# Two graph layers on one core: x·W0a taken ahead of the tiles, x·(W0b+1)+b between them, other edge values, one search for foreign entries per group

## The reference

```
deg = sum(adj, axis=1)
y   = concat([adj @ x / deg, x], axis=1) @ W0 + b
x1  = layernorm(x + y)                      # over the 128 columns, no gain, no offset
h   = x1 @ W.T
e   = (h @ a[:128])[:, None] + (h @ a[128:])[None, :]
p   = softmax(where(adj == 0, -inf, e), axis=1)
out = layernorm(x1 + p @ h)
```

## Time and profile before

| what | value |
|---|---|
| median of 3 runs | 1074.1 us |
| the profiled execution: its own time, its span | 1073.98 us, 1072.3 us |
| its mean granted TensorE clock | 0.993 |
| TensorE busy | 998.3 us (93%), 8777 instructions |
| VectorE, ScalarE, GpSimd busy | 728.6, 601.0, 310.3 us |
| adj loads | 36864 packets, 268.45 MB |

### The profile page before, as it was taken

One profiled execution on the slowest core, in us unless ns is written; L12 is line 12 of the kernel. 1 busy time (PEld: TensorE's weight loads), 2 busy tenths in 40 slices (PEclk: granted clock), 3 DMA queues, 4 the chain that ended last, 5 costly groups with the idle time before them and its releaser, 6 DMA issues.

```text
span 1072.3 us, 22059 instructions
## 1 busy us (share of the span) xinstructions
PE 998.3 (93%) x8777; PEld 868.2 (81%) x8777; DVE 728.6 (68%) x1722; ACT 601.0 (56%) x533; POOL 310.3 (29%) x333
## 2 busy tenths in 40 slices
PE   0778888989999999999999999999999999999996
PEld 0566677777888888888888888888888888888885
DVE  4797888888978877777666665555534655656654
ACT  5677788888888778776767675656521100000000
POOL 5445344454544443433333333322000000000000
PEclk9999999999999999999999999999999999999999
DMA  9999999999999999999989888879230022222011
GB/s 324 422 421 420 402 409 416 416 417 422 407 421 412 417 395 396 385 386 364 357 346 330 336 325 322 318 314 360 83 127 7 19 71 85 85 85 72 26 41 32
DMA packets 51594, 305.36 MB, mean 285 GB/s; under 512 B 6560, under 2 KB 7840, under 8 KB 17952
## 3 DMA queue, kind: packets, MB, share of 16 engines
q0 software_dynamic: 36864, 268.45, 63.1%
q1 hardware_dynamic: 12672, 33.06, 8.8%
q10 hardware_dynamic: 1952, 2.39, 0.8%
HBM read 286.29 MB, written 17.59 MB: 283 GB/s over the span
## 4 chain that ended last, share of the span: by engine, by line
PE 81%; DMA 9%; ACT 4%; issue 2%; DVE 2%; POOL 1%; ACTq 0%; DVEq 0%; POOLq 0%
PE ps_agg L315 48%; PE ps_part L315 24%; DMA adj_in<-in_adj_dram,chunk 8%; PE ps_y L315 4%; ACT edges L452 3%; PE ps_y L591 1%; PE ps_y L590 1%; POOL adj_in L1144 1%; DMA x_all<-in_x_dram 1%; PE ps_h L598 1%; DVE edgesT L754 1%; PE ps_catT L579 0%; PE ps_x1T L585 0%; PE ps_catT L580 0%; DVE edgesT L751 0%
## 5 line engine op out<-in xcount | busy, mean ns | idle before, releaser
L315 PE MATMUL ps_agg<-parts,edgesT 128*128 128x257 f16 (+1 forms) x5312 | 616.7, 275 | 34.6 <-DVE edgesT L754 30.9
L315 PEld LDWEIGHTS ps_agg<-parts,edgesT 128*128 128x128 fp8e4 x5312 | 520.6, 98 | 119.2 <-DVE edgesT L754 35.7
L452 ACT ACTIVATE edges<-adj_in 128x4096 fp8e4<-128x4096 int32 x126 | 455.4, 3614 | 32.5 <-DMA adj_in<-in_adj_dram,chunk 31.8
L1144 POOL DMA_INDIRECT adj_in<-in_adj_dram,chunk x256 | 260.9, 1019 | 440.3 <-ACT edges L452 387.5
L315 PE MATMUL ps_part<-parts,edgesT 128*128 128x258 f16 x1664 | 194.6, 273 | 0.0
L315 PEld LDWEIGHTS ps_part<-parts,edgesT 128*128 128x128 fp8e4 x1664 | 162.7, 98 | 22.7
L763 DVE SCALAR_TENSOR_TENSOR stray<-edgesT,stray 128x1024 uint32<-128x1024 uint32 x128 | 158.4, 1238 | 0.5
L522 ACT ACTIVATE std<-mean_var,eps 128x1 f32<-128x1 f32 x64 | 18.9, 295 | 204.0 <-DVE mean_var L977 204.0
L458 ACT ACTIVATE catT<-ps_catT 128x256 f32<-128x256 f32 x64 | 24.6, 384 | 159.2 <-PE ps_catT L580 145.0
L751 DVE STREAM_TRANSPOSE edgesT<-edges 128x512 uint32<-128x512 uint32 x128 | 89.9, 702 | 16.6 <-ACT edges L452 13.4
L315 PE MATMUL ps_part<-parts,packed 128*128 128x258 f16 x836 | 96.4, 273 | 0.0
(11 more groups left out here) (100 smaller groups left out, 696.9 us busy)
## 6 DMA issues: line engine op xcount, KB each, us to landing
adj_in<-in_adj_dram,chunk POOLq DMA_INDIRECT x256, 8.8
out_dram<-edges SPq DMA_DIRECT2D x60, 64.0 KB, 2.9
partial_sums<-partial SPq DMA_DIRECT2D x13, 258.0 KB
adj_in<-partial_sums SPq DMA_DIRECT2D x13, 258.0 KB, 6.0
packed_adj<-packed SPq DMA_DIRECT2D x3, 1024.0 KB
x_all<-in_x_dram SPq DMA_DIRECT2D x8, 256.0 KB, 8.4
x_all<-in_x_dram ACTq DMA_DIRECT2D x8, 256.0 KB, 8.9
adj_in<-packed_adj SPq DMA_DIRECT2D x2, 1024.0 KB, 6.8
```

Of the source, the lines that this page charges most:

```text
L315: done = eng.matmul(bank[:, 0:cols], rows[:, n // BYTES, n % BYTES, :], moving[:, n, :], start=(n == first), stop=(n == last))
L452: act.activation(edges[:, half, :, :], adj_in[:, n % SLOTS, :, :], ACT.Copy, scale=2.0 if t % GROUP == GROUP - 1 else 1.0, saturate=False) ...
L1144: pool.indirect_dma_start(adj_in[:, n % SLOTS, r, :], None, adj_chunks, bass.IndirectOffsetOnAxis(chunk[:, 0:1], 0), element_offset=first_ ...
```

## The change

1. `parts0` holds the split of 4096·u, u = x·W0a, in place of x. Ahead of the tiles, for each of 16 groups j of four blocks: four transposes of x (`transpose_x`), one copy by ScalarE (`copy_xT`), four products with W0a (`dense`), the high part by ScalarE (`split_u`), the low part by VectorE (`split_u_lo`).
2. v = x·(W0b+1)+b takes x's place in `x_all`. Groups 0 and 1 are made ahead (`dense_self`, `keep_v`), groups 2 to 15 in the odd tiles 1 to 27: four transposes ahead of first_layer(t), four products behind it, a ScalarE copy and a VectorE addition.
3. Per tile, transpose_cat, the catT copy, project and add_bias are gone. z = (agg + low part + v) comes in two VectorE instructions straight from `ps_agg`; all row work is one tile earlier.
4. An edge is 128.0, or 192.0 in every fourth tile. Kept bits are 0x10, 0x20, 0x40 and 0x04; bits 0x8B are kept along in `packed`, and are searched for only there, once per group (2 instructions in place of 8). Every tile is packed at full width; the stores keep their sizes. The unpack of every fourth tile shifts and masks.
5. The first adj tile is converted and transposed after steps 10, 12, 14 and 15 of the work ahead. GpSimd begins to load adj when the first quarter of x has landed. The first four blocks of x and W0 are loaded first; VectorE transposes both halves of a tile together at the head of its step; extremes of u are taken in tiles 40 to 52.

```diff
+        FIRST_AFTER = [10, 12, 14, 15]
+        AHEAD = 2
+        def late_group(t):
+            j = (t + 3) // 2
+            return j if t % 2 == 1 and AHEAD <= j < GROUPS else None
...
         @block.scalar
+            for j in range(GROUPS + 1):
+                if j < GROUPS:
+                    copy_xT(j)
+                if j > 0:
+                    split_u(j - 1)
+                if j in FIRST_AFTER:
+                    convert_first(FIRST_AFTER.index(j))
             act.wait_ge(s_w1T, 1)
...
-                if on(t, 1):
-                    copy_catT(t - 1)
-                if on(t, 3):
-                    copy_x1T(t - 3)
+                if on(t, 2):
+                    copy_x1T(t - 2)
+                if late_group(t) is not None:
+                    copy_late_xT(late_group(t))
...
-                if on(t, 2):
-                    deviation(t - 2)
+                if on(t, 1):
+                    deviation(t - 1)
...
         @block.tensor
+            for j in range(GROUPS + 1):
+                if j < GROUPS:
+                    transpose_x(j)
+                if j == 1:
+                    pe.wait_ge(s_const, 16)
+                if j > 0:
+                    dense(j - 1)
+                if 0 < j <= AHEAD:
+                    dense_self(j - 1)
...
             def first_layer(t):
                 pe.wait_ge(s_trh, 2 * t + 2)
-                wait(pe, s_aggr, t - 1)
+                wait(pe, s_z, t - 1)
+                if t == 0:
+                    pe.wait_ge(s_lo0, GROUPS)
...
-                if on(t, 1):
-                    transpose_cat(t - 1)
-                if on(t, 3):
-                    transpose_x1(t - 3)
+                if on(t, 2):
+                    transpose_x1(t - 2)
+                if late_group(t) is not None:
+                    late_transpose_x(late_group(t))
                 first_layer(t)
-                if on(t, 1):
-                    project(t - 1)
-                if on(t, 3):
-                    hidden(t - 3)
+                if on(t, 2):
+                    hidden(t - 2)
+                if late_group(t) is not None:
+                    late_dense_self(late_group(t))
...
         @block.vector
             def step(t):
-                if on(t, 0):
+                if on(t, 0) and t > 0:
                     transpose_half(t, 0)
+                    transpose_half(t, 1)
                 if on(t, 1):
                     degree(t - 1)
+                    residual_lo(t - 1)
+                    residual(t - 1)
...
                 if on(t, 0):
-                    check_and_pack(t)
+                    pack(t)
+                if on(t, 1) and (t - 1) % GROUP == GROUP - 1:
+                    check((t - 1) // GROUP, 0)
+                if on(t, 2) and (t - 2) % GROUP == GROUP - 1:
+                    check((t - 2) // GROUP, 1)
+                if late_group(t) is not None:
+                    keep_v(late_group(t))
...
         @block.gpsimd
-            pool.wait_ge(s_x[1], 16 * NQ)
-            for n in range(SLOTS):
+            pool.wait_ge(s_x[0], 16 * NQ)
+            for n in range(2 * TILES):
                 load_half(n)
```

More of the change, by code:

```diff
@@ L438, in _ @@
[L438 to L441, removed]
-            act.wait_ge(s_fill, 1)
[L443 to L446, removed]
+                    first = 1 if s == 0 else 0
@@ L452, in convert @@
                 act.activation(edges[:, half, :, :], adj_in[:, n % SLOTS, :, :], ACT.Copy,
[L453 to L458, removed]
+                               scale=EDGE[t % GROUP], saturate=False).then_inc(s_conv, 1)
             def copy_x1T(t):
@@ L567, in first_layer @@
                 pe.wait_ge(s_trh, 2 * t + 2)
-                wait(pe, s_aggr, t - 1)
[L569 to L580, removed]
+                wait(pe, s_z, t - 1)
+                if t == 0:
+                    pe.wait_ge(s_lo0, GROUPS)
+                if t == 1:
+                    pe.wait_ge(s_vkept, AHEAD)
+                contract(pe, ps_agg[t % 2], edgesT[:, t % 2, :], parts0[:, :, 0:2 * F + 1],
+                         range(NBLK), 0, NBLK - 1).then_inc(s_agg, 1)
             def transpose_x1(t):
@@ L757, in check_and_pack, with pack @@
+                words_transposed(t, 2 * half + 1).then_inc(s_trh, 1)
+            def pack(t):
                 g, c = t // GROUP, t % GROUP
                 dve.wait_ge(s_trh, 2 * t + 2)
-                width = TW // CHECKS
-                def check(part):
-                    wait(dve, s_check, CHECKS * t + part)
-                    dve.scalar_tensor_tensor(stray[:, :], edgesT[:, t % 2, part * width:(part + 1) * width],
-                                             every_byte(0xFF ^ EDGE[c]), stray[:, :],
-                                             ALU.bitwise_and, ALU.bitwise_or).then_inc(s_check, 1)
@@ L767, in check_and_pack @@
-                check(0)
-                words = slice(bands_of(g) * P, TW)
-                bits = edgesT[:, t % 2, words]
-                word = packed[:, g % 2, words]
+                bits, word = edgesT[:, t % 2, :], packed[:, g % 2, :]
                 if c == 0:
                     wait(dve, s_pkst, 16 * (g - 1))
-                    dve.tensor_single_scalar(word, bits, every_byte(BIT[c]), ALU.bitwise_and).then_inc(s_pack, 1)
+                    wait(dve, s_check, CHECKS * (g - 1))
+                    dve.tensor_single_scalar(word, bits, every_byte(KEPT[c] | FOREIGN), ALU.bitwise_and)\
+                        .then_inc(s_pack, 1)
@@ L790, in mean @@
-            def mean(t):
-                dve.wait_ge(s_aglo, t + 1)
-                wait(dve, s_catT, t - 1)
-                dve.scalar_tensor_tensor(agg[:, t % 2, :], ps_agg[t % 2][:, 0:F], rcount[:, :], agg_lo[:, 0:F],
-                                         ALU.mult, ALU.add).then_inc(s_aggr, 1)
-            def residual(t):
-                dve.wait_ge(s_y, t + 1)
-                dve.wait_ge(s_xb, t + 1)
+                if t % GROUP == 0:
+                    dve.wait_ge(s_vkept, t // GROUP + 1)
@@ L1028, in judge @@
                 dve.tensor_scalar(flag[0:1, :], verdict[0:1, 3:4], 1.0, None, ALU.add).then_inc(s_flag, 1)
+            for j in range(GROUPS + 1):
+                if j > 0:
+                    split_u_lo(j - 1)
+                if 0 < j <= AHEAD:
+                    keep_v(j - 1)
+                if j in FIRST_AFTER:
+                    transpose_first(FIRST_AFTER.index(j))
             for t in range(TILES):
@@ L1033, in _ @@
             step(TILES)
+            check(GROUPS - 1, 1)
             unpack(1)
-            step(TILES + 1)
             unpack(2)
```

314 lines of the change are left out of this document (195 added, 119 removed).

## The result

Forecast: 1055 us. Measured: a median of 1089.11 us (four runs, 1086.98 to 1092.72) against 1073.29 for the kernel before (a median of four runs), ratio 1.0144 with the 95% interval [1.0107, 1.0181]. The change makes the kernel slower by 15.8 us. The forecast has the wrong sign and the time lies outside its range.

A forecast was written before the change was run, and what follows sets the result against it. Loads were taken to bound tiles 0 to 29, TensorE tile 30 to the tail's end. 1073.98 - 18.8 (A) - 3.6 (B) - 1.0 (C) + 4 (D) = 1054.6, said as 1055 us; range 1047.5 to 1066.

The forecast's parts named there:

- Price of an instruction: On TensorE, each instruction costs 0.1118 us, from tile 43's 12.19 us for 109 instructions.
- term A: TensorE in tiles 36 to 63: six instructions fewer per tile, 0.671 us each, 18.8 us gained.
- Term C: Head of the tail: three transposes and three products, 9 instructions, go; 1.0 us gained.
- Term B: Tiles 29 to 36 become load-bound at 10.63 us per load, so tile 36 begins 3.6 us sooner; bounds 0 and 4.5.
- the loads set tiles up to 36: After the change, tiles 28 to 35 become load-bound and the border to TensorE-bound tiles moves to tile 36.
- sign of being wrong: Tiles before 28 further apart than 10.8 us with VectorE's edgesT as releaser, or idle TensorE after tile 36.
- Sums: Load-bound tiles: a load priced at 10.63 us, with an upper bound of 4.5 us gained at 421 GB/s.
- Term D: Start: work ahead delays first_layer(0) by 10 us and empties the load queue; 4 us lost, bounds 0 and 12.
- At nothing: Checks, packs, ScalarE copies, add_bias and the unpack shift count nothing; VectorE is at 41 or 34 of 50 us.
- New waits: Load-bound tiles: deviation(t-1) between ScalarE's two conversions never waits; the step fits by 2.7 us.
- The clock: Cold TensorE at the start: 64 products take 10.18 us against 7.33 later.
- The slower rival: Transposes wait behind pack, check and keep_v; load-bound tiles take about 1 us more, 28 in all; 1083 us, chance 0.07.

The follow-up runs named there:

- e2: Changed kernel with keep_v of late groups one step later, behind the next tile's transposes and row work on VectorE; 1077.62 us.
- e7: e6 with the first layer's layernorm square root replaced by a copy, so both table loads per group go too; 1059.09 us.
- e3: Changed kernel with both edits: bias loaded right behind W0, and keep_v of late groups one step later; 1068.4 us.
- e1: Changed kernel with the bias loaded right behind W0, ahead of the rest of x; 1078.22 us.
- e5: e2 with keep_v of groups 0 and 1 behind the whole work ahead, bias load left where the changed kernel has it; 1066.35 us.
- e6: e5 with tile 0's four quarters converted after steps 6, 8, 10 and 12 of the work ahead; 1064.18 us.
- e8: e6 with the next tile's first-half conversion ahead of both copies in ScalarE's step; 1062.72 us.
- e9: e8 with the work ahead's xT copies on VectorE and tile 0's quarters converted after steps 7, 9, 11 and 13; 1065.23 us.
- e10: e8 with tile 0's quarters converted after steps 6, 8, 9, 10 and tile 1's first half after step 13; 1061.38 us.
- e4: Kernel before with part 4 alone: new edge values, full-width packing, one search per group, shift in every fourth unpack; 1072.23 us.

## Why the prediction was wrong, step by step

- **Price of an instruction and term A:** right. From tile 36 to the end the changed kernel takes 18.5 us less than before; terms A and C said 19.8. Tiles of group 10 are 0.67 us shorter.
- **Term B (3.6 us gained) and "the loads set tiles up to 36":** failed. 9 to 36 took 13.2 us more than before, not 3.6 less. Two things the step left out: keep_v's wait (e2: 10.9 us of the stretch), and the chain of the group step (e7: 7.9 us between two traces, 5.1 between the medians; e7 leaves out a part of the chain, and what the wait for h_row costs by itself was not measured). With both out, e7's 288.5 meets the 289.3 of the forecast, so the load time of 10.63 us itself was right. The prediction's own sign of being wrong came true: tiles 9 to 28 begin 11.5 us apart in the mean, with edgesT as the releaser. The pace was uneven already in the kernel before, first_layer of tile 24 on TensorE and the next two of ScalarE's rows:

```profile
290.97 7.34 PE L315 MATMUL ps_agg<-parts,edgesT 128*128 128x257 f16 x64 [0.63 <-DVE edgesT L754]
...
295.50 1.28 ACT L473 ACT_TABLE_LOAD   x1
...
297.52 3.62 ACT L452 ACTIVATE edges<-adj_in 128x4096 fp8e4<-128x4096 int32 x1 [0.43 <-DMA adj_in<-in_adj_dram,chunk]
```

  Tile 25 followed 11.56 us later, not the mean of 10.76. I read the mean and took it for the pace of every tile. It was still the load that came last there: the conversion behind the root waited 0.43 us for it, so the chain was that near to being the bound. In e3 the same conversion waits for nothing.
- **Sums:** TensorE's own 10.6 us per tile in group 8, which term A gives, was left out where a load was priced lower. With it term B's upper bound of 4.5 us (421 GB/s) is 4.0. That does not change the forecast.
- **Term C:** within the 1.3 us by which terms A and C together missed.
- **Term D (4 us lost, 0 to 12):** failed. Tile 9 came 24.0 us late. 11.5 of that is the bias wait (e1), 3.7 keep_v in the tiles up to 9 (e2). Together they took off 13.0 (e3), so 11.0 are left. The rest of the estimate was too good as well: in e5, which has the change's own conversion steps and neither wait, half 3 is issued at 34.43, where the term had its slot free at 31.2, and tile 9 starts 7.7 us late; with the conversions sooner, e6 and e8 still start tile 9 at 136.23 and 135.85, 5.8 and 5.4 us after before, against 4. The estimated 0.62 us of ScalarE per 128x512 was right (0.58 to 0.61 measured). No row shows the 0.05 us between ScalarE's instructions and the 0.3 us of hand-overs: in the changed kernel the instructions of 0.6 us that wait for nothing start 0.49 us apart (35.49 and 35.98 us), and ScalarE waits 0.24 us for TensorE in a group without a conversion. Where the remaining 5.4 us arise is open: e9 and e10 moved the copies and the slots and did not move tile 9 forward.
- **"At nothing":** nearly. VectorE has work to spare, but this was the wrong question. I compared its busy time with the span and so did not see that it can be late while it is idle. The search alone gained 2.4 us (e4).
- **"New waits":** the step that failed. It looked at deviation(t-1) alone. That wait is harmless, as said: the root of line 528 has no wait for mean_var in the trace. The wait that counts was keep_v's, on both its inputs, 80.3 us in all; taking it away gave 20.7 us of time (e3). A second one, weighted_hi's on h_row, was overlooked too. A wait is an added instruction of the queue it stands in, and I had worked out what queues behind deviation but not behind keep_v, which the slower rival itself named as work.
- **The clock:** the prediction reckoned with cold products at the start alone (10.18 us for 64 of them) and put no number on the products behind a later stall. In 100 to 150 us the mean granted clock is 0.85, and tile 20 took 8.97 us at 0.81 after an idle time of 2.07. With e2's edit the first stretch has 0.98. The slow tiles stand behind stalls, but the length of the stall does not decide: tile 16 took 7.34 us at 1.00 behind the same 2.07, and in the kernel before tiles 6 and 10 took 8.97 at 0.81 behind 0.73 and 1.33. Nor was tile 0 warm behind the work ahead, as term D had it: in the changed kernel it took 9.59 us behind 2.31 us of idle TensorE.
- **The slower rival (1083, 0.07)** had the place: the transposes behind pack, check and keep_v. That its 1083 lies near is luck: it had 28 us in the load-bound tiles, where 9 to 36 lost 13.2, and 4 at the start, where 24.0 were lost. It was to decide by VectorE's work growing. The work shrank (34.13 us of 50 in 300 to 350, where the earlier trace rows have 41.45); 5.6 us of waiting in the same queue did it. I gave it 0.07 because I priced work and not waits.

## What to carry to other kernels

For each instruction that a change adds, ask what it waits for and what stands behind it in its queue, and do so for every input: the place of an add of 0.7 us, and of the load behind it, made the difference of 20.7 us between a slower and a faster kernel (e3). Where a mean pace is read from a periodic pipeline, look at one whole period and at what comes last in each of its steps: the long tile in four waited for its load in the kernel before and for ScalarE's chain in e3. And a DMA share of 1.01 does not say that the loads bind (405 GB/s in e6 and 419 in e7, at 1.01 in both); compare the bytes per second with the best stretch.

## What was new about the hardware

A small broadcast load (the bias, 64 KB) took 21.4 us to land when it was issued behind x and 1.8 us ahead of the first indirect loads of adj, 18.5 to 22.3 in e2 and e5 to e10, which have it at the same place, and 7.1 and 6.3 when issued at 2.3 us (e1, e3); before, it took 11.3. Its bytes are the same in all of them; whether what stands ahead of it or what runs beside it makes the difference, no run separates. With idle times of some 2 us once in two tiles the mean granted clock of 100 to 150 us was 0.85, and first_layer of the tile behind such an idle time took 8.76 to 10.20 us in ten tiles of twelve, at granted clocks of 0.83 to 0.70, and not 7.32. The table load took 1.28 us, with 0.02 us of idle ScalarE on either side (e3). A DMA share of 1.01 went with 386 GB/s (the changed kernel, 400 to 425 us) and with 421 (the kernel before, 25 to 50 us).
